# A fused attention and expert layer on one core: a new load order and new places for five pieces of the start-up

## What is computed

```python
x = x + attention(layernorm(x), ctx, mask)          # q = ln(x) @ Wq + bq; softmax over 64 keys; @ Wo + bo
xm = mix(layernorm(x))                              # three-tap mix along the sequence, per channel
h = einsum('bsd,pdm->bspm', xm, W1) + b1            # nine experts, 256 -> 64
paths = einsum('bspm,pmd->bspd', h, W2) + b2        # 64 -> 256
idx = argmax(tanh(xm @ Wo1 + bo1) @ Wo2 + bo2)      # one expert for each token
x = x + layernorm(layernorm(x) + paths[idx]) * gamma + beta   # in outline
```

## Time and profile before

| what | value |
|---|---|
| time, median of three runs (lowest, highest) | 345.53 us (343.94, 347.05) |
| the profiled execution, its own time | 345.07 us |
| its span in the profile | 343.3 us |
| busy: PE, DVE, ACT, POOL | 305.2, 275.8, 177.4, 188.2 us |
| PE busy by fortieth of the span (8.6 us), first seven | 1, 5, 9, 8, 7, 8, 9 tenths |
| mean granted TensorE clock | 0.988 of full speed |

### The profile page before, as it was taken

How to read it: one execution, slowest core, us unless ns; L and a number is a source line. 1 busy time by engine, 2 the same in 40 slices (tenths; PEclk the granted TensorE clock), 3 DMA queues, 4 the chain that set the end, 5 groups by cost and what they waited for, 6 DMA issues and landing times.

```text
span 343.3 us, 6997 instructions
## 1 busy us (share of the span) xinstructions
PE 305.2 (89%) x2700; PEld 225.3 (66%) x2700; DVE 275.8 (80%) x624; ACT 177.4 (52%) x275; POOL 188.2 (55%) x226
## 2 busy tenths in 40 slices
PE   1598789689999999999999999999999998799980
PEld 1574364456579667876679576976787578667980
DVE  1776898998499797989798979987697867778866
ACT  1354824725843677258653785377425753266400
POOL 0163202672494399728882699528962976173053
PEclk9999999999999999999999999999999999899997
DMA  7932200010020010200120010001000010001003
GB/s 220 236 79 77 76 2 3 0 64 15 3 77 1 2 61 2 78 1 3 61 78 2 1 63 2 0 3 48 15 2 1 3 63 0 0 2 61 3 0 122
DMA packets 20570, 13.14 MB, mean 38 GB/s; under 512 B 10097, under 2 KB 20410, under 8 KB 20538
## 3 DMA queue, kind: packets, MB, share of 16 engines
q1 hardware_dynamic: 18898, 12.14, 12.0%
q10 hardware_dynamic: 1640, 0.57, 0.7%
HBM read 8.51 MB, written 4.19 MB: 37 GB/s over the span
## 4 chain that ended last, share of the span: by engine, by line
PE 72%; DVE 15%; ACT 5%; issue 4%; POOL 2%; DMA 2%; DVEq 0%; SPq 0%; ACTq 0%
PE ps L437 15%; PE ps L442 7%; PE ps L685 6%; PE ps L603 6%; PE ps L690 5%; PE ps L686 5%; PE ps L585 4%; PE ps L560 4%; PE ps L579 4%; DVE mx L1160 3%; PE ps L667 2%; PE ps L652 2%; DVE osb L1187 2%; PE ps L563 2%; POOL hml L1520 2%
## 5 line engine op out<-in xcount | busy, mean ns | idle before, releaser
L1463 POOL TENSOR_TENSOR rs<-ve,halfneg 128x4 f32<-128x4 f32 x24 | 26.9, 1120 | 97.9 <-DVE ve L1123 97.9
L871 ACT ACTIVATE e<-ps 128x1024 f32<-128x1024 f32 x32 | 31.0, 1023 | 16.4 <-PE ps L567 16.4
L1160 DVE TENSOR_REDUCE mx<-ps 128x16 f32<-128x1024 f32 x32 | 38.0, 1217 | 0.3 <-PE ps L535 0.3
L685 PE MATMUL ps<-w2h,hmh 128*128 128x256 f32 (+1 forms) x140 | 35.6, 289 | 0.0
L686 PE MATMUL ps<-w2l,hmh 128*128 128x256 f32 (+1 forms) x140 | 34.7, 283 | 0.0
L1520 POOL TENSOR_TENSOR hml<-hs,hmh 128x512 fp32r<-128x512 f32 x24 | 30.0, 1274 | 5.3 <-ACT hmh L932 5.3
L922 ACT ACTIVATE hs<-ps,b1s 128x512 f32<-128x512 f32 x28 | 19.3, 689 | 24.6 <-PE ps L442 24.5
L1509 POOL TENSOR_TENSOR y<-xh2f,gms 128x256 f32<-128x256 f32 x28 | 22.2, 823 | 17.4 <-DVE xh2f L1132 17.4
L603 PE MATMUL ps<-wo,osb 128*128 128x256 f32 x128 | 31.4, 391 | 0.0
L437 PE MATMUL ps<-xmh,w1h 128*128 128x512 f32 x80 | 27.7, 428 | 3.0 <-DVE xmh L1239 2.2
L1280 DVE TENSOR_TENSOR hs<-hs,ps 128x512 f32<-128x512 f32 x28 | 18.6, 682 | 13.7 <-PE ps L667 13.7
(11 more groups left out here) (163 smaller groups left out, 767.1 us busy)
## 6 DMA issues: line engine op xcount, KB each, us to landing
xin<-in_x SPq DMA_DIRECT2D x8, 512.0 KB, 3.7
out<-y SPq DMA_DIRECT2D x7, 512.0 KB, 2.8
min_<-in_mask_Bx1xSxS_ik SPq DMA_DIRECT2D x8, 128.0 KB, 4.4
hs<-in_L_ffn_W SPq DMA_DIRECT2D x2, 288.0 KB
hs<-in_L_ffn_W SPq DMA_DIRECT2D x1, 512.0 KB
out<-xin SPq DMA_DIRECT2D x2, 256.0 KB, 2.2
cst<-in_constants SPq DMA_DIRECT2D x1, 384.0 KB, 7.0
e<-in_ctx ACTq DMA_DIRECT2D x1, 256.0 KB, 5.2
```

Source lines behind the costliest of these rows:

```text
L685: nc.tensor.matmul(o, L.hi(m, r)[:, ks], w2h[0:r, m, :], start=(m == 0), stop=False)
L871: nc.scalar.activation(e[:, 2 * i:2 * i + 2, :], ps[:, bank:bank + 2, :], ACT.Exp).then_inc(s_e, 1)
L1160: v.tensor_reduce(mx[:, k, :].rearrange("p (a h) -> p a h", a=2), ps[:, bank:bank + 2, :].rearrange("p a (h s) -> p a h s", s=SK), AX.X, A ...
L1463: g.tensor_tensor(ln[7][:, :], ln[6][:, :], halfneg[:, :], ALU.pow).then_inc(s_r, 1)
```

## The change

1. **Loads.** SP issues x(0,0) first, then the identity, the context and the mask. The context leaves ACT's queue, and ACT issues the load of Wq last and only after x(0,0) has landed.
2. **Steps 1 and 2.** The query of chunk (0,1) moves on PE from behind step 1's last scores to between the two parts of step 2's transposed scores. On DVE its second remainder `xTl` moves behind the split of the maxima.
3. **Expert weights.** ACT splits them behind the layernorm of (1,0) in step 2, not ahead of its second exponentials. Their remainders and the memset behind them go from DVE to POOL; W2's wait for the maxima of (0,1).
4. **Step 3.** On PE, `t2` of (0,0) and the second part of the transposed scores come ahead of the query of (1,0). Its rounding goes from DVE to ACT.
5. **POOL in step 3.** `rstd2(0,1)` moves ahead of `add_beta(0,0)` and `add_bo(1,0)`, and also waits for the maxima of (1,0).

```diff
@@ sync
+            load(xin[:, 0], xr[:, 0, 0], s_x[0])
             load(cst[:, C_ID:C_D4], consts[:, C_ID:C_D4], s_ident)
-            load(xin[:, 0], xr[:, 0, 0], s_x[0])
+            load(ctx_in, ctx.rearrange("b s d -> s b d"), s_ctx)
             load(min_[:, 0], mr[:, 0, 0], s_m[0])
@@ tensor
-                if late:
+                if late and f:
                     wq(*front, fb, f)
-                    t2(*late, 6 if f else 0)
+                    t2(*late, 6)
                     scores_transposed(*n, 1, front)
+                elif late:
+                    t2(*late)
+                    scores_transposed(*n, 1, front)
+                    wq(*front, fb)
                 if f:
                     w1(*f, 0)
                     w1(*f, 4)
+                if n == (0, 0):
+                    wq(*front, fb)
...
-                if not n:
-                    wq(*after, fb)
@@ scalar
-            load(ctx_in, ctx.rearrange("b s d -> s b d"), s_ctx)
-            load(wq32, Wq.rearrange("(c p) n -> p c n", p=P), s_wq)
...
+            act.wait_ge(s_x[0], 16)
+            load(wq32, Wq.rearrange("(c p) n -> p c n", p=P), s_wq)
...
+            def q_round(b, j):
+                act.wait_ge(s_q, at(b, NJ * KD, (j + 1) * KD))
+                nc.scalar.activation(qr[:, :, :], q[:, :, :], ACT.Copy).then_inc(s_qr, 1)
...
                     q_copy(*front, 6)
+                    q_round(*front)
...
-                if n and n == (0, 0):
-                    split_ffn_weights()
...
                     layernorm1_apply(*after)
+                if n == (0, 0):
+                    split_ffn_weights()
@@ vector
-                if n and n == (0, 0):
-                    ffn_weights_lo()
...
-                if front:
+                if front and (f or not late):
                     q_round(*front)
...
-                if not n:
-                    x_lo(*after, 6)
...
                         split_max(*front)
+                    if not n:
+                        x_lo(*after, 6)
@@ gpsimd
+            def ffn_weights_lo(front):
+                pool.wait_ge(s_w1h, 1)
+                g.tensor_tensor(w1l[:, :, :], w1_32, w1h[:, :, :].bitcast(F32), ALU.subtract).then_inc(s_w1l, 1)
+                pool.wait_ge(s_w2h, 1)
+                pool.wait_ge(s_nm, at(front[0], NJ, front[1] + 1))
+                g.tensor_tensor(w2l[:, 0:4, :], w2_32[:, 0:4, :], w2h[:, 0:4, :].bitcast(F32), ALU.subtract)
...
+                g.memset(hs[DM:, 4, :], 1.0).then_inc(s_ones, 1)
+                pool.wait_ge(s_ones, 1)
...
                 if n and n[1] == NJ - 1 and not f:
                     early_mixed_lo(n[0])
+
+                    pool.wait_ge(s_nm, at(front[0], NJ, front[1] + 1))
+                    rstd2(*n)
                 if next_f:
                     add_beta(*next_f)
...
-                if n:
+                if n == (0, 0):
+                    ffn_weights_lo(front)
+                if n and (f or n == (0, 0)):
                     rstd2(*n)
```

14 lines of the change are left out of this document (4 added, 10 removed).

## The result

The changed kernel takes 354.21 us (median of 4 runs, 353.35 to 354.51), the kernel before beside it 344.92 us (4 runs, 343.94 to 347.05). The ratio is 1.0268, 95% interval 1.0227 to 1.031: slower by 9.3 us. The prediction had slower, by 5.7 in its sum, at 351.0 with a range from 348.0 to 354.0. The direction and the mechanism that decides came out; the size did not, it lies beyond the range, and two terms of the sum failed. The profiled execution took 354.51 us with a span of 352.7.

What follows compares the result with a forecast made beforehand. PE's work sets the overall pace; PE and DVE hand each other the path in the first steps. Terms -1.6 - 0.4 + 0.2 + 0.5 - 0.8 + 6.3 + 1.5 = +5.7 on 345.07 gave 350.8, stated as 351.0, range 348.0 to 354.0.

Steps and rivals of the forecast that it cites:

- Loads, -1.6: Start: x(0,0) in use 1.8 us earlier, of which 1.6 us is gained, bounds 0.5 to 2.3.
- rival (c): Start: Wq arrives late, each microsecond after 11.3 costing about one; 2 us would give 352.6; chance 0.06.
- Steps 1 and 2, -0.4: Steps 1 and 2: maxima split 1.28 us earlier, but the moved query leaves a gain of 0.4 us (0 to 0.7).
- Weights and step 3, +0.2 and +0.5: Steps 2 and 3: POOL's weight work delays rstd2(0,0) by 0.2 us; the query, no longer hidden, costs 0.5 us.
- rival (b): PE's clock: half speed through the first W1 products, or a second fall in step 3; 352.5 to 354; chance 0.22.
- Split of the maxima, -0.8: Step 3: the split of the maxima gets faster because POOL's adds come later, gaining 0.8 us (0 to 0.8).
- POOL in step 3, +6.3: Steps 3 and 4: POOL's late adds delay the load of x(2,0), stalling DVE, then W1; 6.3 us lost (5.5 to 7.5).
- clock, +1.5: Step 4: TensorE's clock falls after PE idles 7 us, costing 1.5 us, bounds 0.66 and 3.1.
- (a): Step 4: the stall without loss of clock, or a start gaining its full 2.3; 348.6 to 349.3; chance 0.17.
- (e): Steps 4 and 5: part of the stall is recovered, leaving +2 to +3, 347.5; chance 0.08.
- (d): Step 4: not slower, as the load of x(2,0) is hidden; -2.1, giving 343.0; chance 0.05.

Runs made afterwards that it cites:

- e13: Kernel before with SP loading x(0,0) first and Wq issued last, only once x(0,0) has landed; context stays in ACT's queue: 345.68 us, ratio 1.003.
- e1: Changed kernel with POOL's order of before: the eight adds of step 3 again ahead of rstd2(0,1); 345.58 us, ratio 1.0026.
- e3: Kernel before with only the new load order (x first, context on SP, Wq last after x lands): 344.45 us, ratio 0.9989.
- e6: Changed kernel with 28 extra, unread products filling PE's wait ahead of step 4's first W1 product: 352.05 us, ratio 1.0236.
- e5: e4 with ten extra, unread products in PE's wait ahead of the transposed maxima of (0,0): 344.11 us, ratio 0.9993.
- e4: Kernel before with only the moved query and remainders of steps 1 and 2 and the moved expert-weight work: 345.29 us, ratio 1.0008.
- e7: Kernel before with only step 3's new PE order and its query's rounding on ACT: 345.39 us, ratio 1.0044.
- e10: Kernel before with POOL's eight adds moved to the start of step 3 and that step's query rounded on ACT: 343.54 us, ratio 0.9959.
- e2: Kernel before with only POOL's new order in step 3, rstd2(0,1) ahead of the adds: 352.67 us, ratio 1.0227.

## Why the prediction was right, and where its size failed

**Loads, -1.6: failed.** The step that x lands near 5.3 was too careful (4.40), and its reason did not hold: the context left ACT's queue, but SP issued it at 1.76, so it still went beside x. The step that fails is "Wq ... with its own 6.0 us arrives at 11.3": it arrived at 13.4, since its transfer took 9.0 us, behind the small tensors and with an issue of 2.13 us. e13 shows that holding Wq back is enough to take the whole gain, and in e1, e3 and e6, with the same start, it is Wq that the queries wait for (in use at 11.79, 12.69 and 12.68, while the transposition of x started by 10.69). This is rival (c), with 2.1 us: it happened in full, beside the stall, where I had given it 0.06 as if it were one of several exclusive cases. A second step fails in the changed kernel's own profile: the context's copies were to "end before the layernorm's reciprocal", which POOL began at 6.78, and they stood at 10.15, behind 3.00 us of waiting for the mask, which was not in my working at all. This alone kept the transposition of x at 12.14. What came is -0.15: the queries 0.39 late, and 0.54 back from there to the first scores, since before had run more of its query pairs at half speed (1.42 and 1.02 us, here 1.19 and 0.69). By the table of the starts it is +0.3 on the average of four executions against eight.

**Steps 1 and 2, -0.4: failed, +1.23.** The count of the work was right (e5: 9.33 us, predicted 9.53). The sentence "was hidden beside the maxima and is now between the two parts" took from PE the work that had covered the wait for the maxima. PE then idled 2.73 us, and the clock fell, a term that I had put at nothing: 10.79 us against 9.53 on the way to pv, 1.26 of the 1.63 us by which this term is off. The other 0.4 lies ahead: first scores to transposed maxima became shorter by 0.89 and not by 1.28, 0.21 of it since DVE now waits for PE's second scores. I asked for idle gaps in step 3 and step 4, and not here. e4, the slowest of its ten runs, lost 2.7 us to the clock.

**Weights and step 3, +0.2 and +0.5: right, +0.95.** From the second layernorm of (0,0) at 55.00 to the denominators at 66.15 are 11.15 us, before 10.71: 0.44 for the new order, and e7 gives 0.46. The other 0.5 is not POOL being late, as I had it: POOL waited 0.38 us for DVE. DVE's small operations were slower beside the remainders and the memset that POOL had taken over (0.42 and 0.47 us, where 0.17 is usual), 0.44 us up to the variance:

```profile
52.30 0.42 DVE L1115 TENSOR_TENSOR su<-st 128x12 f32<-128x12 f32 x1
...
52.84 0.47 DVE L1118 TENSOR_SCALAR mu<-su 128x4 f32<-128x4 f32 x1
...
53.67 1.02 POOL L1461 TENSOR_TENSOR rs<-ve,halfneg 128x4 f32<-128x4 f32 x1 [0.38 <-DVE ve L1123]
```

The fall of the clock that rival (b) named in step 3 happened in the profiles of e1 and e6 and not in that of the changed kernel.

**Split of the maxima, -0.8: right, -0.82,** and e10 repeats it without the stall.

**POOL in step 3, +6.3, and clock, +1.5: right.** Against the maxima's split, SP's issue is 8.8 us later than before (11.69 us behind it instead of 2.91), and I had said some 9. W1 is 7.28 us later for 7.1 predicted. The load goes out 85.21 - 78.00 = 7.21 us behind rs (7.1 predicted: 83.8 - 76.73), lands 3.63 later (3.7), and W1 follows the statistics after 3.32 (3.26). DVE idled 6.47 and not 8.1 us only since its second layernorm took 3.04 instead of 1.38 beside the adds; it was waiting anyway, so this changed nothing. The clock cost 1.61 by e6, less the recovered wait. Of the Trainium skill, page "TensorE: Matmul & The Clock Gate", section "What's actually happening", the rule was that the throttled clock is the default, and activity releases it. The trace agrees: behind 6.63 us of idling PE came back at half speed, with 1.19, 1.05, 1.05 and 1.04 us for the first four pairs of products and 0.65 for the fifth. From the first pair to the fifth it took 3.54 us instead of 1.97, so the four slow pairs cost 1.6 us. That is near my estimate from the earlier trace rows, 1.5, and not the 3.1 us of two whole W1 products.

**Rivals.** (a) and (e), less than the forecast, did not happen: nothing of the stall came back later. (d) is refuted by the result and by e2. Of (b), PE did come back at half speed, but for four pairs only, which is the forecast's own price, and there was no second fall in step 3; a fall of the same size came instead in step 2, which no rival named. (c) happened. Neither kind was an alternative to the forecast: both are additions to it. With 1.5 us for one more fall and the 1.6 at which I had priced (c) it is 351.0 + 1.5 + 1.6 = 354.1. By treating them as exclusive I cut the range at 354.0. That the changed kernel landed 0.2 us beyond this edge and not inside it is chance, since its four runs lie from 353.35 to 354.51; that its two failed terms were off by 3.1 us together is not.
